# Cross-attention block with a ternary feed-forward layer: last tiles, opening and all cross-partition maxima rearranged

## The reference

```
q = layernorm(x) @ w_q;  k = ctx @ w_k;  v = ctx @ w_v          (per batch)
scores = q @ k.T / sqrt(512), causal;  attn = softmax(scores)
x = x + tanh(g_xattn) * (attn @ v)
h = gelu(layernorm(x) @ ternary(W1).T + b1)                      (2048 wide)
x = x + tanh(g_ffn) * (h @ ternary(W2).T + b2)
ternary(w) = clip(round(w / mean|w|), -1, 1)
```

## Time and profile before

| | us |
|---|---|
| median of 3 runs | 1773.81 (1772.19 to 1775.87) |
| the profiled execution | 1774.8 |
| its span, first to last instruction | 1773.0 |
| TensorE busy | 1651.3 (93%) |
| VectorE busy | 863.9 (49%) |
| ScalarE busy | 658.1 (37%) |
| GpSimd busy | 304.0 (17%) |
| mean granted TensorE clock | 0.970 |

### The profile page before, as it was taken

The page is one execution under the profiler, slowest core; times in us unless marked ns, Lnnn a source line. Parts: engine busy times, 40 slices in busy tenths (PEclk is TensorE's granted clock), DMA queues, the critical chain, the costliest instruction groups (busy, mean ns, idle before and its releaser), DMA issues.

```text
span 1773.0 us, 24221 instructions
## 1 busy us (share of the span) xinstructions
PE 1651.3 (93%) x8448; PEld 826.3 (47%) x8448; DVE 863.9 (49%) x1575; ACT 658.1 (37%) x1032; POOL 304.0 (17%) x339
## 2 busy tenths in 40 slices
PE   4699999999999988777699999999999999999999
PEld 1355555565555544433244444444444444444444
DVE  3655656565566554546334434444444444444432
ACT  1223232424233343321244444444444444444443
POOL 1111111111111111111021112211122111221110
PEclk8799999999999998988899999999999999999999
DMA  5245463545545375454322211222112222122210
GB/s 184 71 100 143 98 144 94 138 102 134 104 94 150 90 203 151 131 143 106 82 49 65 66 59 33 61 65 65 59 25 69 65 62 62 24 71 62 64 41 24
DMA packets 261651, 157.52 MB, mean 89 GB/s; under 512 B 222416, under 2 KB 222416, under 8 KB 260432
## 3 DMA queue, kind: packets, MB, share of 16 engines
q1 hardware_dynamic: 261008, 156.31, 34.0%
q10 hardware_dynamic: 576, 0.27, 0.1%
HBM read 70.53 MB, written 33.55 MB: 59 GB/s over the span
## 4 chain that ended last, share of the span: by engine, by line
PE 63%; issue 13%; DVE 12%; DMA 4%; SPq 3%; ACT 3%; POOL 1%; DVEq 0%; POOLq 0%; ACTq 0%
PE t_ps L848 13%; PE e_ps L942 12%; PE s_ps L942 12%; PE v_ps L848 11%; PE o_ps L917 5%; PE s_ps L868 4%; PE t_ps L887 3%; PE v_ps L905 3%; DMA w_in<-in_w1T 2%; SPq L277 2%; DVE v_s L811 2%; DVE cmax L592 2%; DVE negmax L677 1%; ACT p_s L460 1%; DVE w_s L759 1%
## 5 line engine op out<-in xcount | busy, mean ns | idle before, releaser
L785 DVE SCALAR_TENSOR_TENSOR v_s<-g,sc,v_s 128x512 f16<-128x512 f32 x256 | 247.6, 968 | 467.5 <-ACT v_s L517 464.0
L942 PE MATMUL e_ps<-w_s,v_s 128*128 128x512 f16 x1024 | 265.5, 379 | 0.8
L942 PE MATMUL s_ps<-w_s,v_s 128*128 128x512 f16 x1024 | 262.8, 379 | 0.0
L848 PE MATMUL v_ps<-ctx_s,w_s 128*128 128x512 f16 x1024 | 243.6, 381 | 8.9 <-DVE w_s L759 8.9
L848 PE MATMUL t_ps<-ctx_s,w_s 128*128 128x512 f16 x1024 | 243.2, 380 | 0.0
L905 PE MATMUL v_ps<-wv_s,ctx_s 128*128 128x512 f16 x768 | 192.5, 404 | 51.3 <-DVE v_s L719 43.2
L868 PE MATMUL s_ps<-ctx_s,tT 128*128 128x512 f16 (+3 forms) x1152 | 202.3, 331 | 21.4 <-DVE tT L697 14.2
L917 PE MATMUL o_ps<-v_s,pT 128*128 128x512 f16 x864 | 199.9, 383 | 5.0 <-DVE v_s L719 5.0
L887 PE MATMUL t_ps<-xnT,a_s 128*128 128x256 f16 x1536 | 183.5, 277 | 22.6 <-ACT a_s L500 18.6
L517 ACT ACTIVATE v_s<-g,sc 128x512 f16<-128x512 f32 x256 | 184.6, 721 | 8.3
L455 ACT ACTIVATE p<-s_ps,ebias,esc 128x128 f32<-128x128 f32 (+3 forms) x64 | 53.1, 830 | 339.5 <-DVE ebias L683 339.5
(11 more groups left out here) (89 smaller groups left out, 1238.4 us busy)
## 6 DMA issues: line engine op xcount, KB each, us to landing
x_ring<-in_x SPq DMA_DIRECT2D x64, 256.0 KB, 2.8
raw<-in_ctxT SPq DMA_DIRECT2D x8, 2048.0 KB, 8.0
out_y<-x_ring SPq DMA_DIRECT2D x64, 256.0 KB, 2.2
raw<-out_y SPq DMA_DIRECT2D x64, 256.0 KB, 3.2
out_y<-v_s SPq DMA_DIRECT2D x64, 256.0 KB, 2.1
w_in<-in_w1T SPq DMA_DIRECT2D x16, 512.0 KB, 4.3
w_in<-in_w2T SPq DMA_DIRECT2D x16, 512.0 KB, 4.6
xnT<-xn_s SPq DMA_TRANSPOSE x128, 2.5
```

The source lines that it names most:

```text
L785: v.scalar_tensor_tensor(out=g_s[:, f % 4, LO], in0=g32[:, f % 2], scalar=col(C_SG), in1=g_s[:, f % 4, HI], op0=ALU.mult, op1=ALU.subtract ...
L848: last_mm = mm(h_ps[f % 2], w1_s[:, c, (f % FC) * P:(f % FC + 1) * P], yT[:, (f // FC) % 2, a, c, :], start=(a == HI and c == 0), stop=(a ...
L942: last_mm = mm(y_ps[i], g_s[:, f % 4, a, i * P:(i + 1) * P], w2_s[:, f, :], start=(f == 0 and a == HI), stop=(f == FC - 1 and a == LO))
```

## The change

**Maxima.** No `partition_all_reduce` is left. For a context batch VectorE takes the larger of the two half maxima (ccol), multiplies an identity matrix with it (dg, 128x128), and TensorE multiplies a matrix of ones with that (`spread_ctx`, one float32 matmul 128x128 into the new bank m_ps), so that every partition holds all 128 maxima; VectorE reduces that row. TensorE does the spread in slot 3 of a batch between the scores and the A product. w_v and b1 go the same way (128x256), the sums over |W| by a product of ones with a column.

**Scale of A.** It came from the maximum of the finished product. It now comes from a bound: the sum over the four chunks of the products of the two weights' row maxima, summed over partitions by TensorE (BOUND), known before the product is finished.

**Opening.** w_k, w_v and the small inputs are issued by ScalarE's queue. TensorE does ten small matmuls on the matrix of ones first; the last two chunks of A are done output block by output block; the A products of tiles 0 to 3 follow one another, the second in o_ps. VectorE's and ScalarE's opening is written out by hand.

**Every slot.** VectorE's lower part of v now stands ahead of the output update. The output product waits for the output update of the tile before by its own semaphore.

**Last 16 slots.** A slot's weight loads are issued one slot earlier; the plan of chunks changes; a second ternary chunk also stands ahead of the output update. The first three hidden products wait for W1 only.

**Feed-forward.** Four h_ps banks (m_ps and o_ps join), TensorE three steps ahead; the layer norm of the next group one step earlier.

The diff, cut to its core:

```diff
-        W_PLAN = {NT - 15: "SSS", NT - 14: "SSS", NT - 13: "SSS", NT - 12: "SS", NT - 11: "TS", NT - 10: "TS",
-                  NT - 9: "TS", NT - 8: "TS", NT - 7: "TS", NT - 6: "TT", NT - 5: "TT", NT - 4: "TT", NT - 3: "TT",
-                  NT - 2: "TT", NT - 1: "T"}
+        W_PLAN = {NT - 15: "SS", NT - 14: "SSS", NT - 13: "SSS", NT - 12: "TSS", NT - 11: "TSS", NT - 10: "TSS",
+                  NT - 9: "TSS", NT - 8: "T", NT - 7: "T", NT - 6: "T", NT - 5: "T", NT - 4: "TT", NT - 3: "TT",
+                  NT - 2: "TT", NT - 1: "TT"}
-        LN_STEPS = (2, 4, 7, 10)
+        LN_STEPS = (1, 3, 6, 9)
...
                     for m, (at, _, _) in enumerate(W_STEPS):
-                        if at == t:
+                        if at == t + 1:
                             load_weights(m)
-                sp.wait_ge(o_done, t)
+                sp.wait_ge(o_done, t + O0)
...
-                if reduce_ctx:
-                    g.partition_all_reduce(call[:, :], cmax[:, :], P, RMAX).then_inc(ctx_max_all, 1)
...
+            def bound_product():
+
+                dve.wait_ge(wqk_max, DC)
+                linked(v.tensor_tensor(wmp[:, :], wmx[:, 0], wmx[:, 1], ALU.mult))
+                v.tensor_reduce(wbound[:, :], wmp[:, :], AX.X, ALU.add).then_inc(a_bound, 1)
...
+            def ctx_diagonal(batch):
+
+                dve.wait_ge(ctx_max, batch + 1)
+                v.scalar_tensor_tensor(out=ccol[:, :], in0=cmax[:, 0:1], scalar=TINY, in1=cmax[:, 1:2],
+                                       op0=ALU.max, op1=ALU.max).then_inc(ctx_col, 1)
+                dve.wait_ge(ctx_col, batch + 1)
+                v.tensor_scalar(dg[:, 0], ident[:, :], ccol[:, :], None, ALU.mult).then_inc(ctx_diag, 1)
...
                 for m, n in terns[:1]:
+                    ternary(m, n)
+                if not last or t + 1 < NT:
+                    v_lower(it, s)
+                for m, n in terns[1:]:
                     ternary(m, n)
                 if s >= 1:
...
                         if c == 2:
                             ins.then_inc(ctx_max, 1)
+                            ctx_diagonal(batch)
...
-                if f >= 2:
-                    pe.wait_ge(g_act, F - 1)
+                if f >= 4:
+                    pe.wait_ge(g_act, F - 3)
...
+            def spread_ctx(batch):
+
+                pe.wait_ge(ctx_diag, batch + 1)
+                mm(MAXES[:, 0:P], ones[:, :], dg[:, 0], start=True, stop=True).then_inc(ctx_max_all, 1)
...
+                if s > 0 and ctx_step(s) == 3 and (not last or t + TB < NT):
+                    spread_ctx(it * 2 + s // TB + 1)
...
-                    pe.wait_ge(w_ternary, NW)
+                    pe.wait_ge(w_ternary, NW // 2)
                     hidden(0, 0, 0)
                     hidden(1, 1, 0)
+                    hidden(2, 2, 0)
...
-                    pe.wait_ge(v_split, t + 1 if not last or t < NT else NT)
-                    if last and t == NT:
-                        pe.wait_ge(o_done, NT - 1)
+                    pe.wait_ge(v_split, t)
+                    pe.wait_ge(o_done, t + O0 - 1)
...
+            pe.wait_ge(consts, 1)
+            for _ in range(WARM):
+                mm(m_ps[:, 0:P], ones[:, :], ones[:, :], start=True, stop=True)
+            for c in range(2):
+                for m in range(DC):
+                    product(m, (c,))
+            for m in range(DC):
+                product(m, (2, 3)).then_inc(a_mm, 1)
+                if m == 0:
+                    pe.wait_ge(a_bound, 1)
+                    mm(BOUND, ones[:, :], wbound[:, :], start=True, stop=True).then_inc(a_bound_all, 1)
+            pe.wait_ge(w_diag, 2)
+            mm(MAXES, ones[:, :], dg[:, :, :].rearrange("p w n -> p (w n)"), start=True,
+               stop=True).then_inc(wmax_all, 1)
+            t_product(0, -2)
+            t_product(0, -1)
+            spread_ctx(0)
+            v_product(0, -1)
+            slot(0, 0)
```

More of the change, by code:

```diff
@@ L203, in gated_block @@
         PV0 = 2
+        O0 = 1
         def p_turned_by(it, s):
@@ L432, in _ @@
             a = nc.scalar
+            for c in range(DC):
+                act.dma_start(wqk_in[:, 1, c], wkT[:, c]).then_inc(w_qk_in[c], 16)
+            act.dma_start(wv32, wv).then_inc(w_v_in, 16)
             act.dma_start(col(C_G0), g_xattn.partition_broadcast(P)).then_inc(small_in, 16)
@@ L738, in slot @@
                                     ALU.add).then_inc(w_total, 1)
-                for m, n in terns[1:]:
-                    ternary(m, n)
             def ternary(m, n):
@@ L760, in ternary @@
                                        op0=ALU.is_gt, op1=ALU.subtract).then_inc(w_ternary, 1)
[L762 to L774 removed]
+            first_rows(0)
+            weights_max(0)
+            weights_max(1)
+            first_rows(1)
+            weights_max(2)
+            weights_max(3)
+            bound_product()
+            scale_product()
+            dve.wait_ge(consts, 6)
+            wv_max()
+            product_lower()
+            scale_wv()
+            for h in range(2):
+                dve.wait_ge(ctx_in0[h], 16)
+                ins = ctx_half(h)
+            ins.then_inc(ctx_max, 1)
+            ctx_diagonal(0)
+            t_lower(0, -2)
+            scale_first_ctx()
+            wv_lower()
+            ctx_lower(0, 0, 0)
+            t_lower(0, -1)
+            first_rows(2)
+            first_rows(3)
+            v_lower(0, -1)
+            ctx_lower(0, 0, 1)
+            gates()
+            first_rows(4)
+            slot(0, 0)
+            ctx_lower(0, 0, 2)
+            ctx_lower(0, 0, 3)
             with dve.Fori(0, TURNS - 1) as it:
@@ L826, in _, with product @@
             mm = nc.tensor.matmul
-            def product(c):
-                pe.wait_ge(w_qk_in[c], 32)
-                for m in range(DC):
+            def product(m, cs):
+                for c in cs:
+                    pe.wait_ge(w_qk_in[c], 32)
                     last_mm = mm(a_ps[m], wqk_in[:, 0, c, m * P:(m + 1) * P], wqk_in[:, 1, c, :],
                                  start=(c == 0), stop=(c == DC - 1))
-                    if c == DC - 1 and m % 2:
-                        last_mm.then_inc(a_mm, 1)
+                return last_mm
             def hidden(F, f, g):
@@ L855, in slot @@
                 i = s % TB
-                if s >= 0 and (not last or t < NT):
+                if not last or t < NT:
                     par, pr, q = (s // TB) % 2, (s // 2) % 2, s % 2
```

336 lines of the change are left out of this document (180 added, 156 removed).

## The result

| | before | after |
|---|---|---|
| median of runs, us | 1773.0 (1769.67 to 1775.87, 4 runs) | 1709.01 (1706.08 to 1712.73, 4 runs) |
| the profiled execution, us | 1774.8 | 1707.6 |
| its span, us | 1773.0 | 1705.8 |
| TensorE busy, us | 1651.3 (93%) | 1639.9 (96%) |
| mean granted TensorE clock | 0.970 | 0.986 |

What follows compares the result with a forecast made beforehand. TensorE was taken as the bound from 107 to 618 us and in the feed-forward, with waits in opening and last slots. From 1774.8 us, -17.7 + 18.2 - 58.0 - 17.7 - 5.7 gave 1693.9, median 1693; range 1662 to 1718.

Steps and rivals of the forecast that it cites:

- The loop: Loop: removed GpSimd reductions save 8.3 us, five spreads cost 5.3 us each: +18.2 us.
- Rival A: Spread costs less: diagonal as early as before, no clock fall, 18 us less, 1675; without stall 1661; chance 0.18.
- The last 16 slots: Last 16 slots: loads a slot earlier end most waits and low clock; 5.3 and 3 us stay: -58.0 us.
- The hand-over: After the last scores: hidden products waiting for W1 only cover the last tile's chain: -17.7 us.
- mask to the end of the lower part of p ... 10.8 us after the scores: Hand-over: last tile's chain of 5.5 us, transposes 2.6, landing 2.7, done 10.8 us after the scores.
- The opening: Up to the first batch's A product of slot 3: GpSimd reduction waits and two maxima go: -17.7 us.
- The bound that named tiles 2 and 3: Opening: gain of 12 us if these tiles' late statistics hold TensorE up by two transposes (2.60 + 2.7 us).
- The feed-forward: Feed-forward stage: TensorE three steps ahead removes 0.38 us at each of 15 group ends: -5.7 us.
- C: Opening gains 5 instead of 17.7 us, as the rows' transposes queue behind bulk loads: 1706; chance 0.08.
- D: Last slots: early loads wait in SP's queue with transposes behind them, 11.8 us a slot: 1867; chance 0.03.
- B: Last slots: VectorE becomes the bound, 16 ternary chunks of 2.1 us fall on TensorE: +33, 1726; chance 0.11.
- E: Opening: ten small warm-up products raise TensorE's clock, saving 3.0 us: 1690; chance 0.3, on top of any other case.

Runs made afterwards that it cites:

- the run that took the wait away: Changed kernel with the rows of tiles 2 and 3 normalised right behind the first batch's scale, ahead of the lower parts: 1709.37 us (0.9629).
- the comparison that is clear of noise: Ten warm-up products put back into the fastest version (late spread, VectorE's old loop order, tail moves): 1668.02 us (0.9394) against 1663.60 (0.9360).

## Why the prediction was right, and where it was off

**The loop** was right in mechanism and place, and near in size. Stalls were forecast at 3.7 us and are 4.1 on average (five of them, 20.3 us); the clock at 1.4, and four of the five A products took 4.08 to 4.45 us instead of 2.78. Undoing the reordering gave 12 us, moving the spread 21, and both together 33, where the sum had 32 for six spreads (6 x 5.3). Rival A (the spread costs less in the change as it is) fell: no stall of the loop was as short as its 2.1 us. With the old order five spreads gave 12 us, 2.3 each, where A had 3.0.

**The last 16 slots** were forecast at 173.4 and took 178.3. The step "one more spread (5.3), and 3 us for the slots with two chunks" had to hold 13.2 us. The spread cost 3.36 of wait and 2.5 of clock (an A product of 5.32 us). The two that it lacked have nothing to do with full slots: the total that TensorE waits 2.17 us for, and the 2.59 us of wait and 1.7 of clock at tile 60's scores, because the rows for the feed-forward had been loaded too late (VectorE stands 3.38 us for them at 755.84, ahead of tT). That the ternary chunks cost TensorE nearly nothing in this stretch was right, though most of them took VectorE 3.1 us each and not 2.1. That the load's lead is what matters was right and stronger than put: both experiments on it, from either side, move 54 and 66 us.

**The hand-over** has the largest error for its size: -13.8 instead of -17.7. The step that failed is "mask to the end of the lower part of p ... 10.8 us after the scores": it let VectorE be free when the last scores ended. It was 2.7 us late (804.68 against 801.95), with slot 62's second chunk ahead of the output update, and the output product of tile 62, put at 4.5 us, waited 2.80 and ran 6.38. Of the 2.7 us, 1.4 are slot 62's two chunks at 5.5 us instead of the 4.1 of the earlier trace rows. The fourth hidden product came 20.8 us after the scores, not 16.8. The gain is also less the work of the step that the term named. The kernel before with the early load alone, whose hidden products still wait for all the weights, has a hand-over of 21.7 us, 11.1 of the 13.8 us; what the wait for W1 only would give without the early load no run shows.

**The opening** gave 15.0 of 17.7. The bound that named tiles 2 and 3 came true in its wait (9.82 us), but not in its price: up to tile 2's scores the opening is 84.01 - 65.93 = 18.1 us shorter, all that was forecast, and the run that took the wait away gained nothing that can be told. From there to the A product of slot 3 it is 3.1 us longer (84.39 - 65.93 = 18.5 against 99.39 - 84.01 = 15.4). The step that failed is a term put at nothing: the prediction says that the first batch's spread lies in the opening and has no price for it there. It is 1.7 us, the wait of 1.34 and 0.3 until the A product starts. The other part is the A product of slot 2, which waits 3.86 us for transposes instead of 1.75; tile 2's scores, 1.1 us shorter at the full clock, give some of it back. Why these transposes land later stays open. No run takes apart what the new maxima, the bound and the new order each gave to the 18.1.

**The feed-forward** was exact: 15 x 0.38 = 5.7 forecast, 5.9 by the pieces; with the lead undone the stage is 5.7 us longer, though the whole time does not show it beyond its noise.

**Rivals.** C (a small gain in the opening) and D (the weight ring closing on itself) did not occur, nor did B as a whole; B showed only where two chunks were put into slots 58 to 61. E was wrong with its sign. The Trainium skill ("TensorE: Matmul & The Clock Gate", section "Why this matters for your kernels") advises to warm the engine first, for measuring a matmul; the prediction read that as a rule for the kernel, and by it the one without the warm-up should have been slower. It was 4.4 us faster. The same section of the Trainium skill advises against idle gaps between bursts of matmuls; the trace agrees, as four of five A products behind a stall took 4.08 to 4.45 us instead of 2.78.

## What to carry to other kernels

When a wait moves from an engine that has slack into the queue of the one that bounds the kernel, look for the latest place in that queue that still serves the reader: here a few lines' distance was worth 21 us, and the other engine's order 12 more. A load issued in the slot that uses it makes its user wait each time (57.1 us in ten waits here); issuing it one slot ahead was worth more than everything else in this change. Work that then starts earlier can fall beside another engine's and run longer, so read its duration again. Removing a wait of the bounding engine may only move it, where another engine has the same work left to do; the end of the stage tells. When a sum leaves a cost to another piece, check that the other piece has it.

## What had not been expected of the hardware

- Warming up TensorE by ten small products raised the clock for the first product in some executions (1.98 us for four records) and not in others (3.78), and the kernel without it was faster, by 4.4 us in the comparison that is clear of noise.
- VectorE's L815 took 2.06 to 2.28 us in every chunk where GpSimd's L389 ran beside it, and 1.28 in every other (11 and 5 of 16 in the changed kernel).
- How long TensorE may wait before the clock falls is not one number here. In the changed kernel and in that with VectorE's old order, A products behind waits of 3.52, 2.79, 2.59 and 2.00 us ran in 2.78 us; behind waits of 2.45 and 3.53 they took 4.12 and 4.33. A stall of this length is priced by a mean over many (some 1.3 us), not by a rule.
- A turn of the loop costs TensorE 2.3 to 3.4 us with nothing that the profile shows to wait for, at tile 17's and tile 33's scores, in every trace.
